# Attention scores of a fused attention and expert kernel: from split rows stacked by way of DRAM to plain fp32 in 32-row tiles of the array

## What is computed

```python
def xattn(query, key, values, mask, W_out):      # query = layernorm(x), key = values = ctx
    energy = einsum('nqhd,nkhd->nhqk', q, k)
    energy = where(mask == 0, -1e20, energy)
    attn = softmax(energy / sqrt(512), axis=-1)
    out = einsum('nhqk,nkhd->nqhd', attn, v).reshape(N, Q, 512)
    return out @ W_out.T
x = x + xattn(layernorm(x), ctx, ctx, mask, W_out)
# ffn: z = x @ proj_w.T; q = tanh(z / 0.3); logits from q @ anchors.T; the top 2 of 6 by softmax
#      h = gelu(x @ w1[e]); out = sum over the two of weight * (h @ w2[e])
x = x + ffn(layernorm(x))
```

## Time and profile before

| what | us |
|---|---|
| median of 3 runs (769.19, 769.54, 3418.46) | 769.54 |
| span of the profiled execution | 768.0 |
| PE busy in it | 633.3 |
| PE weight loads | 500.1 |
| DVE busy | 499.0 |
| ACT busy | 356.5 |
| POOL busy | 271.2 |

### The profile page before, as it was taken

How to read it: one execution, slowest core, us unless ns; L and a number is a source line. 1 busy time by engine, 2 the same in 40 slices (tenths; PEclk the granted TensorE clock), 3 DMA queues, 4 the chain that set the end, 5 groups by cost and what they waited for, 6 DMA issues and landing times.

```text
span 768.0 us, 15465 instructions
## 1 busy us (share of the span) xinstructions
PE 633.3 (82%) x4084; PEld 500.1 (65%) x4085; DVE 499.0 (65%) x1037; ACT 356.5 (46%) x675; POOL 271.2 (35%) x393
## 2 busy tenths in 40 slices
PE   3669999999999698899996496999999999999000
PEld 2666666666655276677685395999999988888000
DVE  7458888888877644767696372554555666676465
ACT  3748878787766615655453131333333333333000
POOL 6733444334300024478767700000000232132474
PEclk9989999999999989999996597999999999999655
DMA  5789989999866359589984936555656788887697
GB/s 180 219 251 265 272 256 281 273 271 261 244 200 199 121 185 327 187 313 326 339 338 185 346 99 206 187 185 195 190 189 191 235 273 293 292 279 249 206 292 251
DMA packets 119460, 185.30 MB, mean 241 GB/s; under 512 B 11366, under 2 KB 47206, under 8 KB 119404
## 3 DMA queue, kind: packets, MB, share of 16 engines
q1 hardware_dynamic: 109164, 151.06, 61.2%
q0 software_dynamic: 10240, 33.56, 13.3%
HBM read 102.79 MB, written 81.26 MB: 240 GB/s over the span
## 4 chain that ended last, share of the span: by engine, by line
PE 39%; DMA 15%; DVE 14%; issue 13%; ACT 7%; POOL 6%; SPq 5%; DVEq 1%; POOLq 0%; ACTq 0%
PE ps L1429 4%; DMA y_d<-ysb 4%; PE ps L1372 4%; PE ps L1533 3%; PE ps L1534 3%; PE ps L1535 3%; PE ps L1522 3%; PE ps L1554 3%; PE ps L1556 3%; PE ps L1555 3%; DVE nmax L1004 3%; DVE newton L1016 3%; DMA atL<-att_d 3%; ACT rden L861 2%; ACT lnden L858 2%
## 5 line engine op out<-in xcount | busy, mean ns | idle before, releaser
L762 POOL DMA_INDIRECT yg<-y_d,sidx x64 | 63.2, 988 | 256.2 <-DVE wst L1254 233.2
L930 ACT ACTIVATE xgH<-ps 128x512 fp32r<-128x512 f32 x74 | 44.3, 599 | 121.6 <-PE ps L1522 121.6
L1533 PE MATMUL ps<-w1H,xgH 128*128 x296 | 90.9, 307 | 1.6 <-DVE xgL L1275 1.6
L1372 PE MATMUL ps<-kss,qst 98*128 98x256 f32 x512 | 82.3, 296 | 12.0 <-DVE nmax L1004 9.2
L1004 DVE TENSOR_REDUCE nmax<-ps 128x4 f32<-128x512 f32 x128 | 83.5, 674 | 11.9 <-PE ps L1372 11.9
L1372 PEld LDWEIGHTS ps<-kss,qst 98*128 98x128 f32 x512 | 69.9, 191 | 23.3 <-DVE nmax L1004 17.5
L1535 PE MATMUL ps<-w1L,xgH 128*128 x296 | 84.8, 286 | 0.0
L1534 PE MATMUL ps<-w1H,xgL 128*128 x296 | 84.6, 286 | 0.0
L1288 DVE COPY ysb<-ps 128x512 f32<-128x512 f32 x74 | 51.1, 690 | 44.6 <-PE ps L1556 25.8
L742 POOL DMA_INDIRECT xs_d<-x,place_now x64 | 64.6, 1009 | 21.0 <-issue 20.1
L1275 DVE TENSOR_TENSOR xgL<-ps,xgH 128x512 fp32r<-128x512 f32 x74 | 51.1, 690 | 31.1 <-ACT xgH L930 31.0
(11 more groups left out here) (181 smaller groups left out, 1413.0 us busy)
## 6 DMA issues: line engine op xcount, KB each, us to landing
xg<-xs_d SPq DMA_DIRECT2D x74, 256.0 KB, 3.1
y_d<-ysb SPq DMA_DIRECT2D x74, 256.0 KB, 2.7
qst<-qhi_d SPq DMA_DIRECT2D x64, 256.0 KB, 3.7
xin<-in_x SPq DMA_DIRECT2D x32, 256.0 KB, 4.3
qhi_d<-qth SPq DMA_DIRECT2D x32, 256.0 KB, 4.3
qlo_d<-qtl SPq DMA_DIRECT2D x32, 256.0 KB, 4.5
qst<-qlo_d SPq DMA_DIRECT2D x32, 256.0 KB, 4.4
att_d<-atT SPq DMA_DIRECT2D x32, 256.0 KB, 2.1
```

Of the source, the lines that this page charges most:

```text
L762: nc.gpsimd.indirect_dma_start(yg[:, k, z, :], None, y_d[b], bass.IndirectOffsetOnAxis(ap=sidx[:, k, z:z + 1], axis=0))\
L1372: last = mm(ps[:, B_MX + t % 2, o:o + 2 * keys], qst[0:R_MAX, g, h, t * P:(t + 1) * P], kss[0:R_MAX, stack, c:c + 2 * keys], start=(h % 2 ...
L1533: mm(o, xgH[:, p, c, :], w1h[:, cols], start=(c == 0), stop=False)
```

## The change

It rewrites the attention stage; the middle and the experts stay.

- **Operands.** `xhi`, `xlo`, `qst`, `kss` and the two DRAM tensors go. POOL writes the normalised row `xn` in fp32 (two operations in one instruction), PE transposes it once, ACT copies it to `qT` (three blocks deep), where a group's four heads lie in four strips of 32 partitions.
- **Scores.** Both kinds are plain fp32 matmuls with 32 rows, head h in rows 32h to 32h + 31 of the array. By token: 16 calls of 128 tokens x 128 keys a unit, in two halves (`pair`) of two heads, which alternate between two row tiles and banks 4 and 5. By key: four calls of 512 tokens into banks 0 to 3, and then four more in fp32r that add mask bias and maximum: `selT` picks their rows out of `mT` (10 rows at the start of each strip).
- **Maxima.** DVE takes them per head (128x512 to 128x4 as before). The split, the transposes and the copy to `mT` are made once a block, for 64 columns at once, in every fourth step; PE waits for them between the two by-token halves.
- **Masked keys.** For the maxima a masked key is replaced by a valid one (`kfT`), made in the set-up with fp32 matmuls over a selecting matrix.
- **Newton.** DVE multiplies sum and 1/sum; the rest, 2 - that and the product with 1/sum, moves to POOL (`recip`).
- **Order.** Blocks run in order, batch by batch, all steps are unrolled. The set-up of the keys comes ahead of step 0, W_out's chunks in steps 2 to 5. The lags: by token 5, split of the maxima 9, by key 10, sums and PV 11, division 12.

The set-up's code is left out, and the declarations mostly:

```diff
-    qhi_d = dram("qhi_d", [nblk, kchunks, P, blk], F32)
-    qlo_d = dram("qlo_d", [nblk, kchunks, P, blk], F32)
...
-        xhi = sb("xhi", [P, 2, emb])
-        xlo = sb("xlo", [P, 2, emb])
         xn = sb("xn", [P, 2, emb])
-        qth = sb("qth", [P, 2, kchunks, P])
-        qtl = sb("qtl", [P, 2, kchunks, P])
-        qst = sb("qst", [P, 4, hpg, blk], F32R)
+        qT = sb("qT", [P, 3, kchunks, blk])
-        newton = sb("newton", [P, blk])
+        newton = sb("newton", [P, 2, blk])
+        recip = sb("recip", [P, 2, blk])
-        mhl = sb("mhl", [2 * hpg, 2, blk])
+        mT = sb("mT", [P, 2, blk], F32R)
+        nmax = sb("nmax", [P, 2, 4, HEADS])
+        nmhl = sb("nmhl", [P, 2, 4, P])
+        ctok = sb("ctok", [P, batches, emb])
+        kT = sb("kT", [P, batches, kchunks, P])
+        kfT = sb("kfT", [P, batches, kchunks, P])
+        selT = sb("selT", [P, batches, kchunks, P], F32R)
...
-        B_TH, B_TL, B_MX, B_SC, B_NUM, B_DEN = 0, 1, 2, 4, 6, 7
+        B_SC, B_XT, B_MT, B_MX, B_NUM, B_DEN = 0, 0, 1, 4, 6, 7
+        B_CNT, B_SEL, B_WT, B_FILL, B_KT = 2, 2, 2, 4, 6
...
+        L_LOAD, L_STAT, L_XT, L_TOK, L_MT, L_KEY, L_PV, L_DIV = -2, 0, 1, 5, 9, 10, 11, 12
+        def unit(v):
+            return v // kchunks, v % kchunks
+        def batch_of(n):
+            return n // blk_per_batch
+        def attention_loop(body):
+            for s in range(L_LOAD, ntile + L_DIV):
+                body(s)
...
@@ sync @@
+            def attention(s):
+                w = s - L_LOAD
                 if live(w, ntile):
+                    n, t = w // 4, w % 4
                     after(sp, xn_done, w - 3)
+                    sp.dma_start(xin[:, t, :], x_t[n, t, :, :]).then_inc(x_in[t], 16)
+                if s == 0:
+                    setup()
+                v = s - L_DIV
                 if live(v, ntile):
+                    n, g = unit(v)
                     sp.wait_ge(at_done, v + 1)
+                    sp.dma_start(att_d[n, g, :, :], atT[:, v % 2, :]).then_inc(at_out[g], 16)
...
@@ gpsimd @@
+            def attention(s):
+                d = s - L_DIV
+                if live(d, ntile):
+                    pool.wait_ge(newton_done, d + 1)
+                    after(pool, at_done, d - 1)
+                    nc.gpsimd.tensor_scalar(recip[:, d % 2, :], newton[:, d % 2, :], 2.0, None, ALU.subtract)\
+                      .then_inc(less_done, 1)
+                    pool.wait_ge(less_done, d + 1)
+                    nc.gpsimd.tensor_tensor(recip[:, d % 2, :], recip[:, d % 2, :], rden[:, d % 2, :], ALU.mult)\
+                      .then_inc(recip_done, 1)
+                w = s - L_STAT
                 if live(w, ntile):
+                    n, t = w // 4, w % 4
...
+                    pool.wait_ge(x_in[t], 16 * (n + 1))
+                    after(pool, xt1_ready, w - 1)
+                    nc.gpsimd.tensor_scalar(xn[:, w % 2, :], xin[:, t, :], mv1[:, t, 0:1], rstd1[:, t, :],
+                                            ALU.subtract, ALU.mult).then_inc(xn_done, 1)
+                if (s - L_MT) % kchunks == 0 and live((s - L_MT) // kchunks, nblk):
+                    n = (s - L_MT) // kchunks
+                    pool.wait_ge(mx_done, HEADS * (n + 1))
+                    after(pool, mt_ready, n - 1)
...
+                    nc.gpsimd.tensor_scalar(columns[:, :, :, :, 0].bitcast(F32R), maxima, 1.0, None, ALU.mult)\
+                      .then_inc(nmh_done, 1)
+                    pool.wait_ge(nmh_done, n + 1)
+                    nc.gpsimd.tensor_tensor(columns[:, :, :, :, 1].bitcast(F32R), maxima, columns[:, :, :, :, 0],
+                                            ALU.subtract).then_inc(nml_done, 1)
...
@@ scalar @@
+            def attention(s):
+                v = s - L_KEY
                 if live(v, ntile):
+                    for h in range(hpg):
+                        act.wait_ge(sc_ready, hpg * v + h + 1)
+                        after(act, pv_done, v - 1)
+                        nc.scalar.activation(prob[:, v % 2, h, :], ps[:, B_SC + h, :], ACT.Exp, scale=scale).then_inc(exp_done, 1)
+                w = s - L_XT
                 if live(w, ntile):
+                    n, t = w // 4, w % 4
+                    act.wait_ge(xt1_ready, w + 1)
+                    after(act, sc_ready, hpg * kchunks * (n - 2))
+                    nc.scalar.activation(qT[:, n % 3, :, t * P:(t + 1) * P],
+                                         ps[:, B_XT, :].rearrange("p (k t) -> p k t", k=kchunks), ACT.Copy).then_inc(qT_done, 1)
+                if (s - L_MT) % kchunks == 0 and live((s - L_MT) // kchunks, nblk):
+                    n = (s - L_MT) // kchunks
+                    act.wait_ge(mt_ready, n + 1)
+                    after(act, sc_ready, hpg * kchunks * (n - 1))
+                    nc.scalar.activation(mT[:, n % 2, :], ps[:, B_MT, :], ACT.Copy).then_inc(mt_done, 1)
...
@@ vector @@
+            def maxima(v, pair):
+                n, g = unit(v)
+                for j in range(2):
+                    h = 2 * pair + j
+                    dve.wait_ge(mx_ready, hpg * v + h + 1)
+                    after(dve, nml_done, n - 1)
+                    nc.vector.tensor_reduce(nmax[:, n % 2, :, g * hpg + h],
+                                            ps[:, B_MX + j, :].rearrange("p (t k) -> p t k", t=4),
                                             axis=AX.X, op=ALU.max, negate=True).then_inc(mx_done, 1)
+            def attention(s):
+                w = s - L_STAT
+                if live(w, ntile):
+                    n, t = w // 4, w % 4
...
+                    nc.vector.bn_stats(st1[:, t, :], xin[:, t, :]).then_inc(st_done, 1)
+                d = s - L_DIV
                 if live(d, ntile):
                     dve.wait_ge(rec_done, d + 1)
+                    after(dve, recip_done, d - 1)
+                    nc.vector.tensor_tensor(newton[:, d % 2, :], ps[:, B_DEN, :], rden[:, d % 2, :], ALU.mult)\
                       .then_inc(newton_done, 1)
                 if live(w, ntile):
                     dve.wait_ge(st_done, w + 1)
                     after(dve, xn_done, w - 3)
                     nc.vector.bn_aggr(mv1[:, t, :], st1[:, t, :]).then_inc(mv_done, 1)
+                v = s - L_TOK
                 if live(v, ntile):
+                    maxima(v, 0)
+                if live(d, ntile):
+                    _, g = unit(d)
+                    dve.wait_ge(recip_done, d + 1)
+                    dve.wait_ge(pv_done, d + 1)
+                    after(dve, at_out[(d - 2) % kchunks], 16 * ((d - 2) // kchunks + 1) if d >= 2 else 0)
+                    nc.vector.scalar_tensor_tensor(atT[:, d % 2, :], ps[:, B_NUM, :], -1.0, recip[:, d % 2, :], ALU.mult, ALU.mult)\
+                      .then_inc(at_done, 1)
+                if live(v, ntile):
+                    maxima(v, 1)
...
@@ tensor @@
+            def scores_by_token(v, pair):
+                n, g = unit(v)
+                if pair == 0:
+                    pe.wait_ge(qT_done, 4 * n + 4)
+                    pe.wait_ge(s_kfT, batches)
+                after(pe, mx_done, hpg * v + 2 * pair)
+                for t in range(4):
+                    for j in range(2):
+                        r = (2 * pair + j) * HD
+                        last = mm(ps[:, B_MX + j, t * P:(t + 1) * P], qT[r:r + HD, n % 3, g, t * P:(t + 1) * P],
+                                  kfT[r:r + HD, batch_of(n), g, :], start=True, stop=True)
+                        if t == 3:
+                            last.then_inc(mx_ready, 1)
+            def scores_by_key(v):
+                n, g = unit(v)
+                b = batch_of(n)
+                after(pe, exp_done, hpg * v)
+                pe.wait_ge(qT_done, min(v + L_KEY - L_XT, ntile))
+                pe.wait_ge(mt_done, n + 1)
+                for h in range(hpg):
+                    r = h * HD
+                    mm(ps[:, B_SC + h, :], kT[r:r + HD, b, g, :], qT[r:r + HD, n % 3, g, :], start=True, stop=False)
+                for h in range(hpg):
+                    r = h * HD
+                    mm(ps[:, B_SC + h, :], selT[r:r + R_BIAS + 2, b, g, :], mT[r:r + R_BIAS + 2, n % 2, :], start=False, stop=True)\
+                        .then_inc(sc_ready, 1)
+            def attention(s):
+                k = s - L_KEY
+                if live(k, ntile):
+                    scores_by_key(k)
+                a = s - L_TOK
+                if live(a, ntile):
+                    scores_by_token(a, 0)
+                v = s - L_PV
+                if live(v, ntile):
+                    pe.wait_ge(exp_done, hpg * (v + 1))
+                    after(pe, newton_done, v)
...
+                    last.then_inc(sums_ready, 1)
+                w = s - L_XT
+                if live(w, ntile):
+                    pe.wait_ge(xn_done, w + 1)
+                    after(pe, qT_done, w)
+                    if live(k, ntile):
+                        pe.wait_ge(exp_done, hpg * k + 1)
```

(52 more changed lines are left out.)

423 lines of the change are left out of this document (120 added, 303 removed).

## The result

The changed kernel takes 825.5 us (median) where the kernel before takes 769.4: a ratio of 1.072 (95% interval 1.069 to 1.075), 7.2% slower. The forecast was 757, and its range ended at 822. The profiled execution has a span of 824.0, 56.0 more than before.

The account below looks back on a forecast made before the run. Attention was taken as paced by a ring of ACT, DVE and PE, 6.84 us a step. Its phase falling from 204.3 to 192.3 gave 768.0 − 12.0 = 756.0, median 757.5, taken as 757; range 738 to 822.

Parts of the forecast that it names:

- 28 forecast: Start-up of attention: by-token scores put to start at 28 us.
- rivals 2 and 3: Attention's row tiles load weights one after another (820, chance 0.16), or do not overlap at all (878, chance 0.11).
- rival 1: In attention, the split's wait is mostly hidden: about 15 of 27 us, so 742; chance 0.13.
- the forecast's 192.3: Attention phase from first sums to last atT: 192.3 us, 12.0 less than 204.3.
- The price of GpSimd's one-input operations: GpSimd's one-input 128x512 operations in attention: 0.70 us each, near the memset's 0.53, with 1.29 as upper bound.
- the wait: PE's wait for the maxima's split in every fourth attention step: 3.2 us, making that step 8.9.
- The ordinary step: Attention step without a split: 5.7 us where it took 6.84, paced by a ring through DVE and GpSimd.
- the short steps at the end: Attention steps 37 to 42, without by-token scores, paced by Newton, GpSimd and atT: 3.8 us.
- Rival 4: PE's seven waits in attention cost the clock: 20 us more, 777; chance 0.20, shared with the dear GpSimd.
- the dear GpSimd: A one-input GpSimd operation of 1.29 makes attention steps 6.0 and 9.9: 770; chance 0.20, shared with Rival 4.
- The start-up: Before the first sums: steps 5 to 10 at 5.3 us each, first sums at 62, nothing gained, ± 5.
- PE's own step: PE's work in an attention step: 5.5 us including five mode changes of 0.5 together, before 6.0.

Follow-up runs that it names:

- b2_order: Changed kernel with each by-token half running all four matmuls of one row tile, then the other's, instead of alternating; ratio 1.166 to the kernel before.
- a1: Changed kernel with the maxima's split moved to the head of GpSimd's step, ahead of 2 - d*r and its product; ratio 1.001 to the kernel before.
- a2_dummy: Changed kernel plus four full-width fp32 matmuls in every fourth step, run while PE waits for the split; ratio 1.048 to the kernel before.
- g1_copies: Changed kernel with GpSimd's two one-input 128x512 operations replaced by plain copies, values not the reference's; ratio 1.020 to the kernel before.
- a4_newton_dve: Changed kernel with only the second Newton step moved back from GpSimd to DVE; ratio 1.018 to the kernel before.
- b3_banks: Changed kernel with the second pair of by-token scores using the sums' and PV's banks through step 10; ratio 1.052 to the kernel before.
- e1_startup: b4_all plus full-width fp32 matmuls, three in each of steps 3 and 4, one in each of 5 to 9; ratio 0.961 to the kernel before.
- a5_xn_act: Changed kernel with xn moved from GpSimd to ACT, ahead of qT, Ln and Exp; ratio 1.059 to the kernel before.
- b4_all: b3_banks plus the split heading GpSimd's queue, second Newton step on DVE, xn on ACT behind Exp; ratio 0.963 to the kernel before.

## Why the prediction was wrong

**The frame held.** By-token scores began at 26.93 (28 forecast). Row tiles run side by side: 0.98 for a half, 1.14 for the key quartet (rivals 2 and 3 are out, as b2_order shows too, and rival 1 with them, since no wait was hidden). The first projection follows the last atT as before. DVE waits for GpSimd's product, and PE for nmhl every fourth step, as described. With the split out of the way (a1) the phase is 194.8; the forecast's 192.3 is close only by chance, since that sum held up to 22 us of waits, which a1 has not, and lower prices. It also began with the key scores of step 11, some 2 us ahead of the first sums from which the phase counts (4.2 us in the trace, at the lower clock), and never took that off.

**The price of GpSimd's one-input operations** is the first step that failed: 0.70 taken, at most 1.29 allowed, 1.50 and 2.09 measured. The reason given, that a one-input operation is like a memset because it has one stream a side, is wrong; a copy is like one, arithmetic isn't. The earlier trace rows could have said so. The same tensor_scalar stands there with one column, 0.23, and with 16, 0.28: 0.05 / 15 = 3.3 ns a column, 1.9 us for 512. That is coarse, since the two rows are rounded, but it lies far above my upper bound. I used the nearest size (512 columns of another operation) instead of the nearest operation. Of the Trainium skill's rule (GPSIMD Engine Reference, Engine selection, near line rate with one input) these runs bear out only the copy; the warning on that page, that elementwise work belongs on VectorE, was the part that applied.

With these prices the wait is 4.5 where 3.2 was forecast: on the forecast's scale, from the key scores, the split ended at 8.3 instead of 6.6, and PE was ready at 3.8 instead of 3.5. The ordinary step is 6.04 to 6.30 instead of 5.7, and the short steps at the end 4.9 and more instead of 3.8.

**The clock** is the second. Rival 4 named it, with a chance shared with the dear GpSimd of 0.20, and priced it at 20 us; a2_dummy has 24.6. The size was near enough, but the step that failed was to leave this term out of the sum: PE's waits of 3.91 and 4.54 in the earlier trace rows both have 0.50 behind them, the one in 51:57, the other in 270:275 of the same trace, which I left unread. It belonged in the forecast. The waits of 2.3 and 2.4 in g1_copies and a4_newton_dve, shorter than the 3.2 forecast, cost the clock as well. And the rival gave the two mishaps as alternatives, with 777 and 770. They compound, since the dearer operations lengthen the wait that costs the clock: behind the waits of 2.3 PE worked 5 to 11 us until the full clock was back, behind those of 4.5 it was 8 to 12.

**The start-up** is the third, 11 us beyond the 62 forecast (10 beyond the 62.93 that the total was worked out from). Steps 5 to 10 take 6.97 instead of 5.3 because a half takes 2.08 at the lower clock. I said that the keys' matmuls run at the cold clock before step 1 and then counted the halves at full clock, with no row for it. The trace shows PE at the full clock in between (1.00 in 12:15). It lost it between 15 and 20, where it stands 2.65 and then 3.68 us for GpSimd's xn (matmuls at 16.26 and 21.03). b3_banks and e1_startup show the shared banks and the clock. The price plays in here too: with the copies of g1_copies the by-token scores begin at 21.74 instead of 26.93 and the first sums come at 63.88, 9.1 us sooner. Either edit alone, cheaper operations or more banks (9.6), makes up most of the miss.

**PE's own step** is 5.86, not 5.5. From start to start the groups behind the key scores (0.98 or 0.99, 1.00, 0.59, 1.09, 1.00) are 0.11 to 0.22 longer than my count of their calls, where I had allowed 0.1 a change of mode. In the changed kernel GpSimd was slower still, but in the best versions this is the step.

Of the missing 68 us, then: 24.6 clock in attention (a2), about 31 from longer waits and steps, 10 start-up, 2 behind attention, whose cause stays open. Cut the other way, by g1_copies: 44 us go with the price (35 in the phase, 9 ahead of it; the ratios 1.072 and 1.020 make it 40), 20 of the phase and 1 of the start-up remain with the price right, and the same 2.

## What to carry to other kernels

Before work is moved to another engine, find that engine doing the same operation at any two sizes and take the slope; a row of the right size but another operation is no bound. In an in-order queue, work that another engine waits for goes ahead of work that nobody waits for: the place of one split was worth 53 us here. An operation that waits for another engine, put ahead of work on which that engine in turn depends, closes a ring: it made the step of a5_xn_act 7.29 us. Where PE has to wait some 2 us or more in a stage like this one, count the time behind the wait at the lower clock, unless rows of the same kind of work show a wait of that length without it.

## What the runs showed of the hardware

In steps 11 to 32 PE fell to 1.2 GHz behind every wait for the split of 2.3 us or more (changed kernel, a4_newton_dve, a5_xn_act, g1_copies, b2_order, b3_banks), and behind one of 1.99 (107.33 in b2_order); in step 33 also behind one of 1.67 (259.23 in the changed kernel, 0.53 in 260:265). It did not fall behind those of 1.05 (a2_dummy) and 0.81 (g1_copies, step 33). The length of a single wait doesn't settle it, though. In a5_xn_act the clock fell to 0.50 in 120:122 where the longest wait since 104 was 0.93. And in the middle of b4_all, amid full-width matmuls of 512 columns, this wait left it at 1.00 in 274:280:

```profile
276.99 1.36 PE L1444 MATMUL ps<-ident,x 128*128 128x128 f32 x8 [3.29 <-ACT x L826]
```

How long PE worked until the full clock was back also varied: 8 to 12 us behind the waits for the split in the changed kernel, 5 to 18 in a4_newton_dve, whose order is the same, and 20 to 33 in b2_order, whose by-token calls run on one 32-row tile at a time. In 28:50 of b4_all, all but gapless and mostly 32-row by-token scores, it did not come back at all. With six full-width matmuls of 512 columns in steps 3 and 4 and one (0.96 us) in each of steps 5 to 9, it was at 1.00 from 25 on. So a busy PE is no sign of a PE at the full clock.
